# Block sums as fp16 high and low products, with the pair values split row by row as they arrive

## The reference

```python
block1 = jnp.einsum('bikc,bkjc->bijc', protein_pair, ab)   # i, j: over 256 k
block2 = jnp.einsum('bikc,bjkc->bijc', ab, compound_pair)  # i, j: over 64 k
out = g * (layernorm(block1 + block2, lnc_w, lnc_b) @ as_w + as_b) * z_mask
x = x + out
```

## Time and profile before

| | |
|---|---|
| runs | 1159.89, 1164.69, 1182.2 us; median 1164.69 |
| profiled execution | 1164.22 us, span 1162.4 us, mean granted TensorE clock 0.799 |
| busy share of the span | PE 83%, PEld 66%, DVE 56%, ACT 48%, POOL 50% |
| stage A (projection) | until about 180 us |
| block sums, half 0 / half 1 | 189 to 257 us / 382 to 451 us |
| pipeline, half 0 / half 1 | 258 to 355 us / 452 to 550 us |
| experts | 640 us to the end |

### The profile page before, as it was taken

One profiled execution on the slowest core, in us unless ns is written; L12 is line 12 of the kernel. 1 busy time (PEld: TensorE's weight loads), 2 busy tenths in 40 slices (PEclk: granted clock), 3 DMA queues, 4 the chain that ended last, 5 costly groups with the idle time before them and its releaser, 6 DMA issues. The chain is left out here.

```text
span 1162.4 us, 26502 instructions
## 1 busy us (share of the span) xinstructions
PE 965.9 (83%) x7510; PEld 764.3 (66%) x7511; DVE 656.4 (56%) x2206; ACT 552.2 (48%) x1247; POOL 581.1 (50%) x622
## 2 busy tenths in 40 slices
PE   1999998987995996898382698898898689899995
PEld 1445557984765995475220587787788578888884
DVE  6446762007675202778642577777777466666673
ACT  1335652114442112443410576676677467677773
POOL 2335651004331543876887255564556356656564
PEclk9999997555565555656555799999999899999998
DMA  7436710005560102235342233333333243444441
GB/s 194 133 118 184 217 70 37 1 29 183 175 193 1 37 32 87 79 120 166 122 148 77 73 120 100 114 112 108 107 110 96 77 121 109 124 115 119 117 122 41
DMA packets 111182, 124.56 MB, mean 107 GB/s; under 512 B 22110, under 2 KB 74359, under 8 KB 111131
## 3 DMA queue, kind: packets, MB, share of 16 engines
q1 hardware_dynamic: 91036, 80.92, 24.8%
q0 software_dynamic: 15296, 34.64, 8.5%
q10 hardware_dynamic: 4800, 8.39, 1.9%
HBM read 77.21 MB, written 49.09 MB: 109 GB/s over the span
## 5 line engine op out<-in xcount | busy, mean ns | idle before, releaser
L998 DVE TENSOR_TENSOR AB<-AB 128x512 f16<-128x512 f32 x280 | 191.7, 685 | 55.2 <-ACT AB L662 54.2
L516 POOL DMA_INDIRECT row_dram<-B x140 | 143.0, 1021 | 123.2 <-DVE B L1004 85.2
L516 POOL DMA_INDIRECT out<-B x140 | 143.9, 1028 | 103.9 <-DVE B L1004 57.2
L659 ACT ACTIVATE AB<-ps 128x512 f16<-128x512 f32 x280 | 168.2, 601 | 42.2 <-PE ps L1171 41.3
L1188 PE MATMUL ps<-PPb,AB 128*128 x1120 | 187.4, 221 | 0.0
L1189 PE MATMUL ps<-PPb,AB 128*128 x1120 | 187.0, 221 | 0.0
L662 ACT ACTIVATE AB<-ps 128x512 f32<-128x512 f32 x280 | 169.1, 604 | 0.0
L1169 PE MATMUL ps<-B,PPb 128*128 128x256 f16 x560 | 155.5, 278 | 0.0
L1170 PE MATMUL ps<-B,PPb 128*128 128x256 f16 x560 | 155.5, 278 | 0.0
L1171 PE MATMUL ps<-B,PPb 128*128 128x256 f16 x560 | 155.4, 277 | 0.0
L1191 PE MATMUL ps<-PPb,AB 128*128 x1120 | 155.2, 220 | 0.0
(11 more groups left out here) (225 smaller groups left out, 1988.3 us busy)
## 6 DMA issues: line engine op xcount, KB each, us to landing
B<-row_dram SPq DMA_DIRECT2D x70, 264.0 KB
PPb<-in_L_conv_protein_pair SPq DMA_DIRECT2D x32, 512.0 KB, 4.8
B<-row_dram SPq DMA_DIRECT2D x70, 136.0 KB
rows<-in_x SPq DMA_DIRECT2D x32, 256.0 KB, 2.8
g_dram<-work ACTq DMA_DIRECT2D x32, 256.0 KB, 2.0
work<-g_dram SPq DMA_DIRECT2D x32, 256.0 KB, 2.8
ABT<-in_x SPq DMA_DIRECT2D x32, 256.0 KB, 3.0
row_dram<-work SPq DMA_DIRECT2D x9, 264.0 KB, 2.7
```

The lines of the kernel that those rows point to most:

```text
L516: pool.indirect_dma_start(out_rows if second else row2_dram, bass.IndirectOffsetOnAxis(ap=Rw[:, u, b, at:at + 1].bitcast(u32), axis=0), Rw ...
L659: act.activation(Hp[:, hs, 0, :], ps[HB[hs]][:, :], ACT.Gelu, scale=1.0 / SCALE)
L998: dve.tensor_tensor(Hp[:, hs, 1, :], Hf[:, q, :], Hp[:, hs, 0, :], ALU.subtract).then_inc(h_parts[q], 1)
```

## The change

The products of the block sums are made from fp16 parts: value times 16, rounded to fp16, is the high part; the rest is the low part. All four partial products are summed: the high and low part of the stationary operand follow one another into the same bank, those of the moving operand stand side by side in it, and the eviction adds the two halves.

- `PPb` holds the high and the low part of a half, [2, 128 i, 128] fp16, in the same bytes. So a piece lands in a staging slot first (`PPs0`, four slots beside x in `rows`; for half 1 `PPs1`, two slots in the upper half of `ABT`), ScalarE writes the high part (`pp_high`), VectorE the low part (`pp_low`), both on whole runs. SP waits for a slot (`pp_split`) ahead of the next piece.
- `AB` is split as well: VectorE masks in place, then writes the high part; GpSimd subtracts the low part (`ab_low`) and raises `abm_done`.
- The transposes are fp16, twice as many; ScalarE copies 1024 fp16 at a time. In half 1 it waits for `pp_split` first, since PPs1 lies in ABT.
- The block sums take 16 banks of four channels a half. The stationary operand is `PPh[:, r, :, g * C + channel]`, a step of 256 bytes.
- The eviction is a reduction on VectorE (`evict`). In half 1 the evictions stand between the steps of `choose(0)`, which now runs ahead of the wait for the block sums; `ranks(0)` moves to bank 8; `weights(0)` moves behind ScalarE's copies.

```diff
+        PPh = PPb[:, :, :].rearrange("p a b -> p (a b)").bitcast(f16).rearrange("p (r i q) -> p r i q", r=2, q=IC * C)
+        AB16 = AB[:, :, :, :].rearrange("p h c j -> p (h c j)").bitcast(f16).rearrange("p (h a r d j) -> p h a r d j", h=IC, a=C // 2, r=2, d=2)
+        ABT16 = ABT[:, :, :].rearrange("p a i -> p (a i)").bitcast(f16).rearrange("p (a r i) -> p a r i", a=C // 2, r=2)
+        CP16 = CPz[:, :, :].rearrange("p c j -> p (c j)").bitcast(f16).rearrange("p (c r j) -> p c r j", c=C, r=2)
...
+        PPs0 = rows[:, :, :].rearrange("p j r -> p (j r)")[:, 4096:8192].rearrange("p (s i q) -> p s i q", s=4, i=8)
...
+        PPs1 = ABTf[:, 2048:4096].rearrange("p (s i q) -> p s i q", s=2, i=8)
...
-            def pp_piece(h, n):
-
-                sp.dma_start(PPb[:, bass.ds(n * 8, 8), :], ppv[:, h, bass.ds(n * 8, 8), :]).then_inc(pp_loaded[h], 16)
+            def pp_piece(h, n, slot, done):
+
+                sp.dma_start(slot, ppv[:, h, bass.ds(n * 8, 8), :]).then_inc(done, 16)
...
                 if u % 2:
-                    pp_piece(0, n // 2)
+                    if not isinstance(n, int) or n >= 8:
+                        sp.wait_ge(s.pp_split, n - 7)
+                    pp_piece(0, n // 2, PPs0[:, u // 2, :, :], pp_in0[u // 2])
...
                     if h == 0:
-                        pp_piece(1, n)
+                        sp.wait_ge(s.pp_split, n * 2 + 30 if not isinstance(n, int) or n >= 2 else 32)
+                        pp_piece(1, n, PPs1[:, u % 2, :, :], pp_in1[u % 2])
...
+            def ab_low(q, v):
+                for g in range(2):
+                    n = q * 2 + g
+                    pool.wait_ge(s.ab_hi, n + 1)
+                    at = bass.ds(n % GH * TG, TG)
+                    view = lambda r: AB16[:, bass.ds(n // GH, 1), :, r, :, at].rearrange("p h a d t -> p t (h a) d")
+                    pool.tensor_tensor(view(1), sg[:, g, :, :].rearrange("p t (a d) -> p t a d", d=2), view(0), ALU.subtract).then_inc(s.abm_done, 1)
...
-            pipeline(pool, GROUPS // 2, 2, [(0, rs_x), (2, mask_g)])
+            pipeline(pool, GROUPS // 2, 2, [(0, rs_x), (2, mask_g), (2, ab_low)])
...
-                    pool.wait_ge(s.blk_done, 16)
+                    pool.wait_ge(s.blk_done, 2 * BANKS)
...
-            pipeline(act, GROUPS, 8, [(0, norm_x), (1, zT_copy), (2, sig), (4, g_store)], depth=4)
+            def pp_high(slot, m):
+                return act.activation(PPh[:, 0, bass.ds(m * 8, 8), :], slot, ACT.Copy, scale=PSCALE)
+
+            def pp_high0(n, u):
+                if u % 2:
+                    act.wait_ge(pp_in0[u // 2], (n // 8) * 16 + 16)
+                    pp_high(PPs0[:, u // 2, :, :], n // 2).then_inc(s.pp_hi, 1)
+
+            pipeline(act, GROUPS, 8, [(0, norm_x), (1, zT_copy), (2, sig), (2, pp_high0), (4, g_store)], depth=4)
...
             for h in range(IC):
+                if h:
+                    act.wait_ge(s.pp_split, 64)
                 for m in range(C // 2 // 4):
                     act.wait_ge(s.abT_psum, h * 8 + m + 1)
-                    act.activation(ABT[:, 4 * m:4 * m + 4, :].rearrange("p a i -> p (a i)"), ps[m % 2][:, :], ACT.Copy).then_inc(s.abT_copied, 1)
-                if h == 0:
-                    act.wait_ge(s.cp_done, 2)
-                for m in range(8):
-                    act.wait_ge(s.blk_done, h * 8 + m + 1)
-                    act.activation(B[:, :, 8 * m:8 * m + 8].rearrange("p j c -> p c j"),
-                                   ps[2 + m % 4][:, :].rearrange("p (c j) -> p c j", c=8), ACT.Copy).then_inc(s.blk_copied, 1)
-
+                    act.activation(ABT16[:, 4 * m:4 * m + 4, :, :].rearrange("p a r i -> p (a r i)"), ps[m % 2][:, :].bitcast(f16), ACT.Copy).then_inc(s.abT_copied, 1)
+                if h:
+                    weights(0)
...
+                def pp_high1(n, u):
+                    if h == 0:
+                        act.wait_ge(pp_in1[u % 2], (n // 2) * 16 + 16)
+                        pp_high(PPs1[:, u % 2, :, :], n).then_inc(s.pp_hi, 1)
 
                 pipeline(act, GH, 4, [(0, await_norm), (1, bT_copy), (0, norm_b),
-                                      (6, await_logit), (4, x1T_copy), (6, logit_copy)],
+                                      (6, await_logit), (4, x1T_copy), (1, pp_high1), (6, logit_copy)],
...
-                    i = dve.tensor_tensor(sg[:, u % 2, 2 * q:2 * q + 2, :], v[:, :, C:2 * C], sg[:, u % 2, 2 * q:2 * q + 2, :], ALU.mult)
+                    i = dve.scalar_tensor_tensor(sg[:, u % 2, 2 * q:2 * q + 2, :], v[:, :, C:2 * C], SCALE, sg[:, u % 2, 2 * q:2 * q + 2, :],
+                                                 ALU.mult, ALU.mult)
                 i.then_inc(s.ab_done, 1)
                 dve.wait_ge(s.ab_done, n + 1)
-                dve.tensor_tensor(AB[:, bass.ds(n // GH, 1), :, bass.ds(n % GH * TG, TG)].rearrange("p h c t -> p t (h c)"), sg[:, u % 2, :, :],
+                dve.tensor_tensor(sg[:, u % 2, :, :], sg[:, u % 2, :, :],
                                   Mk[:, bass.ds(n * TG, TG)].rearrange("p (t o) -> p t o", o=1).broadcast_to([P, TG, C]),
-                                  ALU.mult).then_inc(s.abm_done, 1)
+                                  ALU.mult).then_inc(s.ab_masked, 1)
+                dve.wait_ge(s.ab_masked, n + 1)
+                dve.tensor_copy(AB16[:, bass.ds(n // GH, 1), :, 0, :, bass.ds(n % GH * TG, TG)].rearrange("p h a d t -> p t (h a) d"),
+                                sg[:, u % 2, :, :].rearrange("p t (a d) -> p t a d", d=2)).then_inc(s.ab_hi, 1)
+
+            def pp_low(slot, m):
+                return dve.scalar_tensor_tensor(PPh[:, 1, bass.ds(m * 8, 8), :], slot, PSCALE,
+                                                PPh[:, 0, bass.ds(m * 8, 8), :], ALU.mult, ALU.subtract)
+
+            def pp_low0(q, v):
+                dve.wait_ge(s.pp_hi, q + 1)
+                pp_low(PPs0[:, v, :, :], q).then_inc(s.pp_split, 2)
...
             pipeline(dve, GROUPS // 2, 4, [(0, stat_x), (1, norm_x), (3, lambda q, v: ab_x(q * 2 + 1, 1)),
-                                              (1, lambda q, v: norm_group(q, v, 1)), (2, lambda q, v: ab_x(q * 2, 0))])
+                                              (1, lambda q, v: norm_group(q, v, 1)), (2, lambda q, v: ab_x(q * 2, 0)), (3, pp_low0)])
...
-                dve.tensor_copy(CPz[lo:hi, q::2, :], CPraw[lo:hi, :, q::2].rearrange("k j c -> k c j")).then_inc(s.cp_done, 1)
+                raw = CPraw[lo:hi, :, q::2].rearrange("k j c -> k c j")
+                dve.tensor_scalar(CP16[lo:hi, q::2, 0, :], raw, PSCALE, None, ALU.mult).then_inc(s.cp_done, 1)
+            for q in range(2):
+                lo, hi = q * C, (q + 1) * C
+                raw = CPraw[lo:hi, :, q::2].rearrange("k j c -> k c j")
+                dve.wait_ge(s.cp_done, q + 1)
+                dve.scalar_tensor_tensor(CP16[lo:hi, q::2, 1, :], raw, PSCALE, CP16[lo:hi, q::2, 0, :],
+                                         ALU.mult, ALU.subtract).then_inc(s.cp_done, 1)
+
+            def evict(h, m):
+
+                dve.wait_ge(s.blk_done, BANKS * h + m + 1)
+                parts = ps[2 + m % 4][:, :].rearrange("p (c r j) -> p c j r", c=4, r=2)
+                dve.tensor_reduce(B[:, :, 4 * m:4 * m + 4].rearrange("p j c -> p c j"), parts, AX.X, ALU.add).then_inc(s.blk_copied, 1)
...
                     dve.wait_ge(s.tail, tails[0])
+                    for m in between.get(tails[0] - TAIL * b, ()):
+                        evict(1, m)
...
             for h in range(IC):
-                dve.wait_ge(s.blk_copied, 8 * h + 8)
+                if h == 0:
+                    dve.wait_ge(s.cp_done, 4)
+                    for m in range(BANKS):
+                        evict(0, m)
+                else:
+                    choose(0, {2: [0], 4: [1], 6: [2], 8: [3], 10: [4], 12: [5], 14: [6], 16: [7], 19: [8], 20: [9], 21: [10], 22: [11], 23: [12],
+                               24: [13], 25: [14, 15]})
+                dve.wait_ge(s.blk_copied, BANKS * (h + 1))
...
-                pipeline(dve, GH, 4, [(X1LAG, gate_b), ((0, X1LAG), statistics), ((1, X1LAG + 1), deviations)],
+                def pp_low1(n, u):
+                    if h == 0:
+                        dve.wait_ge(s.pp_hi, n + 17)
+                        pp_low(PPs1[:, u % 2, :, :], n).then_inc(s.pp_split, 2)
+
+                pipeline(dve, GH, 4, [(X1LAG, gate_b), ((0, X1LAG), statistics), ((1, X1LAG + 1), deviations), (2, pp_low1)],
                          after=(GH, lambda: choose(1)) if h else None)
-                choose(2 * h)
+            choose(2)
...
                     for a in range(4):
-                        c = 2 * (4 * m + a)
-                        i = pe.transpose(ps[m % 2][:, a * P:(a + 1) * P], AB[:, h, c:c + 2, :].rearrange("p c j -> p (c j)"), ident[:, :])
+                        for r in range(2):
+                            k = (2 * a + r) * P
```

(60 more changed lines are left out.)

22 lines of the change are left out of this document (13 added, 9 removed).

## The result

The changed kernel takes 1240.89 us, median of four runs (1231.82 to 1244.82), against 1169.93 us of the kernel before, run again beside it (four runs, 1159.89 to 1182.2): ratio 1.0626, 95% interval 1.0512 to 1.074, so slower. The forecast was 1178 us with a range of 1140 to 1215: the measured time lies above it. Its profiled execution took 1244.82 us, span 1243.1 us, mean granted clock 0.767.

| from ... to | before | after | difference | forecast |
|---|---|---|---|---|
| start to the first compound pass on VectorE (stage A) | 179.7 | 233.3 | +53.6 | +11 |
| to the first statistics (block sums of half 0) | 78.8 | 50.4 | -28.4 | -42 |
| to choose(0) (pipeline of half 0) | 106.0 | 154.6 | +48.6 | +51 |
| to the first power of half 1 | 88.9 | 93.2 | +4.3 | -6 |
| to the end | 709.0 | 711.6 | +2.6 | 0 |

What follows compares the result with a forecast made beforehand. TensorE was taken as the bound of half 0's pipeline, and busy without a gap in stage A. The terms -42 + 11 + 51 - 6 = +14 us on 1164.2 us gave 1178 us, range 1140 to 1215.

Steps and rivals of the forecast that it cites:

- Part 2: Stage A: VectorE's added work makes it the bound, a two-group step 10.1 us instead of 7.66; +11 us.
- rival 2: Stage A: gaps put TensorE's products back to 1.22 us, up to 37 us on 22 groups; chance 0.15.
- Part 1: Block sums of half 0: fp16 products in 25 us, the whole stretch 37 us in place of 78.7; -42 us.
- rival 1: Block sums: stepped fp16 loads are slow, 1194 us at 0.107 us a load, 1242 at 0.214; chance 0.2.
- the packed row: Block sums: price from the expert layers' packed fp16 products, 0.055 us per 128 columns; 25 us taken, near it.
- Part 3: Pipeline of half 0: VectorE's low part waits for ScalarE's high part, step 9.4 us in place of 5.8; +51 us.
- the landing: Pipeline of half 0: a piece's load is released two steps ahead, 18 us, so its arrival is hidden.
- the first circle: Pipeline of half 0: VectorE waits for ScalarE's high part, itself behind VectorE's b_ready; 3.95 us, then the low part 1.2.
- rival 3: Pipeline of half 0: ScalarE a step ahead hides the wait, about 2 us cost, 1129 us in all; chance 0.15.
- Part 4: Half 1: earlier block sums, but evictions delay choose(0) (tail_done at 45.3 us) and GpSimd's sends; -6 us.

Runs made afterwards that it cites:

- a3: The kernel after, with two useless 256-column products more per group on TensorE in stage A, from the ninth group on; 1210.01 us.
- b1: The kernel before, with eight more multiplications of 256 fp32 values on VectorE per two groups in stage A; 1215.51 us.
- b2: The kernel before, with twelve more multiplications on VectorE a single time in stage A; 1201.74 us.
- c1: The kernel after with the edits of a1, a3 and a4 together; 1184.76 us.
- c3: The kernel after with the edits of c4 and a7 together; 1225.69 us.
- c4: The kernel after with the edits of a6, a3 and a4 together; 1132.32 us, the kernel before beside it 1163.11 us.
- a2: The kernel after, block sums reading 128 neighbouring fp16 values of PPh instead of every 128th (wrong numbers, same products); 1210.03 us.
- a7: The kernel after, split pair values kept channel by channel: products read packed, ScalarE's and VectorE's conversions write with a step of 256 bytes; 1351.52 us.
- a6: The edit of a1 on the kernel after, and SP sends for the piece of pair values ahead of the gates and x; 1194.22 us.
- a1: The kernel after, ScalarE's high part of half 1's pair values at the head of its list in half 0's pipeline, a weaker wait dropped; 1235.85 us.
- a4: The kernel after, all sixteen evictions of half 1 behind choose(0) instead of between its steps, ranks(0) ahead of bank 4; 1208.96 us.

## Why the prediction was wrong

**Part 2, stage A, is the step that failed**: +53.6 us for +11. VectorE became the bound as said, its step even a little shorter (9.50 us for 10.1). In a3, where TensorE kept its pace, the steps were 9.8 to 10.6 us. But the sum priced the lateness at itself, 2.45 us a step, and left TensorE's pace behind a gap as it was. What a gap costs is TensorE's clock: 6.75 us a group in place of 3.83 until the pace returns, 74 us later at the first gap. Twenty-two groups were quick before, under seven after; 15 groups times 2.92 is 44 us, with the two gaps 49 of the 53.6. A late start of the quick pace is not the cause here: it began at 63.4 us, in before at 95.0. This is rival 2, which had 0.15 and a price of up to 37 on top of the 11; its place and cause were right (b1, b2 and a3 show it), the chance was far too low. The argument against it, that TensorE was still quick at 176.79 us, came from a stretch without gaps. In stage A of after and of ten of the kernels run here, each of 23 gaps from 1.30 to 5.28 us in a quick stretch was followed by products at 1.22 us; in a3, c1, c3 and c4 none of the gaps up to 1.13 us was. How the chip decides, and why the quick pace begins at 29 to 138 us in different runs while TensorE is busy throughout, stays open. The Trainium skill, page "TensorE: Matmul & The Clock Gate", section "HAM oscillation — how this bites in real kernels", tells of a kernel whose TensorE falls back to 1.2 GHz at each wait for the next tile's DMA. The gap rows of after agree in kind; there TensorE waited for VectorE and ScalarE, 2.38 and 2.73 us.

**Part 1, block sums: -28.4 for -42.** The products took 36 us, not 25: rival 1 at its lower price (0.107 us a load; measured 0.11). I took the packed row because stepped fp32 records are hardly longer than packed ones. That mean was misread: nearly all of its loads ran at a granted clock of 0.50. Where the clock was 1.00, the trace of before had the step's price too. Windows of half 0's block sums, then their loads, stepped (L1077) and packed (L1074), in the first and in the second window:

```profile
188.90:193.60 4.70, 4.70 (x25) 4.70 (x25) 0.00 (x0) 0.00 (x0) 0.00 (x0) 1.00 0.00 0
197.00:257.00 60.00, 60.00 (x281) 60.00 (x281) 0.00 (x0) 7.22 (x7) 0.00 (x0) 0.50 0.00 1
...
L1077 PEld LDWEIGHTS ps<-AB,PPb 128*128 128x128 f32 x10 | 2.6, 306 | 0.0
L1074 PEld LDWEIGHTS ps<-CPz,ABT 128*128 128x128 f32 x6 | 0.9, 194 | 0.9 <-ACT ABT L573 0.9
...
L1077 PEld LDWEIGHTS ps<-AB,PPb 128*128 128x128 f32 x112 | 30.1, 319 | 0.0
L1074 PEld LDWEIGHTS ps<-CPz,ABT 128*128 128x128 f32 x56 | 14.6, 320 | 0.0
```

At 1.00 a stepped load takes 306 ns and a packed one 194; at 0.50 they are alike, 319 and 320. fp16 does the same (a2 and after): the step shows only at 1.00, the clock that the packed price of 0.055 us assumes. The way to the first product took 13.4 us (11.2): the compound passes needed 13.2, not 9.8, and the first product waited 1.5 for the last. GpSimd's last low parts took 2.50 us each beside these passes, 1.28 without (estimate 0.92). The rule cited in the prediction (the Trainium skill, page "SBUF — State Buffer", section "Door 1: The DMA port swizzle"), that an access which leaves a 16-byte line costs, holds in kind: a2 and a7 agree, on three engines. The size that the prediction read from it, towards 62 us, did not come (36), and the fp32 rows agree with it too, at 1.00.

**Part 3, pipeline of half 0: +48.6 for +51.** Right: step 9.19 us (9.4), the wait where it was put. a6 shows that the wait, and not the conversions, is the cost. What the prediction did not see is the second circle behind it, over SP and the piece (a1); it put the landing down as hidden, which held only while the first circle was there. With both circles gone (a6) the conversions cost 1.8 us over before, the 2 us that rival 3 gave for a hidden wait.

**Part 4, half 1: +4.3 for -6.** The mechanism is right: sends behind the end of choose(0), 36.7 us from the first send to the first power (36.8). Mis-sized is choose(0): 56.0 us to `tail_done`, not 45.3. The stepped loads stretch VectorE's steps; packed (a2) it is 43.5. a4 shows that the sends, not the block sums, set the start of half 1. (The prediction's terms add up to a first power at 82.1 us, not 82.4, which changes nothing.)

**Rival 3** (the wait is hidden) did not come, for the reason given.

**The total.** Rivals 1 and 2 came together, each at a price near its own: 1178 + 10 + 6 + 37 = 1231 us. The prediction gave each a chance by itself and none to both, and its range ended at 1215. That the measured 1241 us is what rival 1 gives for a load of 0.214 us (1242) is chance: the load took 0.11.

## What to carry to other kernels

Where TensorE and another engine take turns and both are nearly full, price extra work on the other engine by what TensorE's clock does behind a gap, not by the work; useless products in the gaps can be cheaper than the gaps. Read a record's duration together with the granted clock of its stretch: here a mean over the slow stretches hid the price of a step. In this kernel the step through the fp16 values was paid by whoever made it, and most by the writers: measure it on the reader and on the writer before choosing. A wait between in-order lists can hide a second one of the same length, as here, so follow the circle once more with the first wait taken away.

## What the runs showed of the hardware

- Stepped stationary operands cost only where the granted clock was 1.00: fp32 loads 306 ns against 194 packed there, 319 against 320 at 0.50 (before); eight fp16 products 0.89 us against 0.44 at 1.00, 0.89 against 0.85 at 0.50 (after, a2).
- A stepped fp16 stationary operand slows VectorE too: multiplications of 512 fp32 values took 1.3 to 2.2 us beside it, 0.69 beside packed products (a2) and 0.69 beside an idle TensorE (after).
- Behind a gap the low pace lasted 74 us in after (81.5 to 155.7) and 7, 20 and 101 us in a2, with TensorE busy all the time.
